# Gated cross-attention with two expert layers: the same calls on five engines in another written-out order

## The reference

```python
x = x + tanh(g_xattn[0]) * L0_xattn(layernorm(x), ctx)
x = x + tanh(g_ffn[0])   * L0_ffn(layernorm(x))
x = x + tanh(g_xattn[1]) * L1_xattn(layernorm(x), ctx, ctx)
x = x + tanh(g_ffn[1])   * L1_ffn(layernorm(x))

# L0_xattn: one head, both directions, and a gate
char2sub = softmax(Qc @ Ks.T / 16) @ Vs
sub2char = softmax(Qs @ Kc.T / 16) @ Vc
gate = sigmoid(concat(char2sub, sub2char) @ Wg.T + bg)
out  = gate * char2sub + (1 - gate) * sub2char
# L0_ffn: the best of 8 experts, each a 256x256 matrix
out  = (x @ expert_w[top1].T + expert_b[top1]) * max(softmax(x @ router_w.T + router_b))
# L1_xattn: 16 heads of 16 with rotary positions on q and k, then Wo
# L1_ffn: the best 2 of 8 experts, gelu(x @ w_fc.T) @ w_proj, weighted by a softmax over the two
```

## Time and profile before

| | before |
|---|---|
| median of three executions | 536.92 us |
| the three | 531.25, 536.92, 536.98 us |
| profiled execution | 531.52 us |
| its span | 530.2 us |
| mean granted clock of PE | 0.941 |
| PE busy | 469.8 us (89%) |
| VectorE, ScalarE busy | 346.1, 335.1 us |
| GpSimd busy | 280.8 us |
| DMA | 65.33 MB |

### The profile page before, as it was taken

One profiled execution on the slowest core, in us unless ns is written; L12 is line 12 of the kernel. 1 busy time (PEld: TensorE's weight loads), 2 busy tenths in 40 slices (PEclk: granted clock), 3 DMA queues, 4 the chain that ended last, 5 costly groups with the idle time before them and its releaser, 6 DMA issues.

```text
span 530.2 us, 11126 instructions
## 1 busy us (share of the span) xinstructions
PE 469.8 (89%) x3888; PEld 413.9 (78%) x3888; DVE 346.1 (65%) x865; ACT 335.1 (63%) x691; POOL 280.8 (53%) x362
## 2 busy tenths in 40 slices
PE   3999999999999674767886799999999999999996
PEld 3999999999888573636664558788788888878896
DVE  5576676787567557552645676868656695976475
ACT  3388788876758223322254578878867768687833
POOL 2236564575533876445366756837668184423154
PEclk9999999999999957777899579999999999999999
DMA  4679600015667415788768225051220602002001
GB/s 144 210 259 385 241 22 2 22 61 159 211 199 209 157 61 174 193 231 263 197 197 207 56 89 152 1 162 42 69 95 1 180 4 101 22 3 83 1 20 41
DMA packets 42635, 65.33 MB, mean 123 GB/s; under 512 B 6098, under 2 KB 23764, under 8 KB 42580
## 3 DMA queue, kind: packets, MB, share of 16 engines
q1 hardware_dynamic: 41044, 60.42, 37.4%
q0 software_dynamic: 1536, 4.20, 2.6%
HBM read 30.13 MB, written 17.43 MB: 90 GB/s over the span
## 4 chain that ended last, share of the span: by engine, by line
PE 61%; SPq 10%; DMA 8%; DVE 6%; issue 6%; POOL 5%; ACT 4%; POOLq 0%; DVEq 0%; ACTq 0%
PE psum L378 13%; PE psum L380 11%; PE psum L379 11%; SPq L2992 7%; PE psum L385 4%; PE psum L606 4%; PE psum L594 4%; DMA xs<-slots_d 3%; PE psum L577 3%; DMA st<-parts 3%; PE psum L543 2%; DMA y_d<-ys 2%; PE psum L510 1%; ACT PT L1346 1%; PE psum L419 1%
## 5 line engine op out<-in xcount | busy, mean ns | idle before, releaser
L2161 DVE TENSOR_REDUCE mpad<-psum 128x4 f32<-128x1024 f32 x64 | 76.4, 1220 | 23.9 <-PE psum L577 23.7
L1346 ACT ACTIVATE PT<-psum 128x1024 f32<-128x1024 f32 x64 | 63.7, 1026 | 17.6 <-PE psum L594 14.5
L2692 POOL TENSOR_TENSOR wA<-stage,wA 128x512 fp32r<-128x512 f32 x32 | 41.2, 1288 | 59.7 <-ACT wA L1393 57.1
L2230 DVE SCALAR_TENSOR_TENSOR xall<-psum,gat,xall 128x256 f32<-128x256 f32 x112 | 46.6, 474 | 9.7 <-PE psum L380 7.3
L577 PE MATMUL psum<-st 48*128 48x256 f32 x256 | 28.8, 331 | 12.3 <-DMA st<-parts 9.6
L378 PE MATMUL psum<-wB,wA 128*128 128x256 f32 x128 | 39.0, 304 | 0.1
L378 PE MATMUL psum<-x4h,wB 128*128 128x256 f32 x128 | 37.9, 296 | 0.1
L606 PE MATMUL psum<-PT,vv 128*32 128x256 f32 x512 | 36.0, 401 | 1.5 <-ACT PT L1346 1.5
L577 PEld LDWEIGHTS psum<-st 48*128 48x128 f32 x256 | 19.7, 202 | 21.9 <-DMA st<-parts 11.1
L2638 POOL TENSOR_SCALAR nm<-mv 128x2 f32<-128x2 f32 x32 | 7.7, 239 | 53.4 <-DVE mv L1926 41.8
L380 PE MATMUL psum<-x4h,wB 128*128 128x256 f32 x128 | 35.8, 280 | 0.0
(11 more groups left out here) (277 smaller groups left out, 1745.4 us busy)
## 6 DMA issues: line engine op xcount, KB each, us to landing
st<-parts SPq DMA_DIRECT2D x96, 128.0 KB, 3.1
wt<-exp_d SPq DMA_DIRECT2D x30, 384.0 KB, 3.9
slots_d<-ys SPq DMA_DIRECT2D x3, 2304.0 KB, 17.5
stage<-mats_d SPq DMA_DIRECT2D x21, 256.0 KB, 3.1
cx<-ctx_d SPq DMA_DIRECT2D x16, 256.0 KB, 4.5
qr<-qp SPq DMA_DIRECT2D x32, 128.0 KB, 2.6
xs<-slots_d SPq DMA_DIRECT2D x30, 128.0 KB, 4.0
y_d<-ys SPq DMA_DIRECT2D x30, 128.0 KB, 3.8
```

Source lines behind the costliest of these rows:

```text
L1346: e.activation(PT[:, i:i + 2, :, :].rearrange("p a k n -> p (a k n)"), ps2("ST", b, j).rearrange("p a n -> p (a n)"), ACT.Exp, scale=0.25) ...
L2161: e.tensor_reduce(mpad[:, :, 0:16].rearrange("p t (o a) -> p t o a", a=8)[:, :, :, j], ps2("max", b, j).rearrange("p o (t n) -> p t o n", ...
L2230: e.scalar_tensor_tensor(out=xall[:, b, t, :], in0=ps("dn", b, x)[:, t * 256:(t + 1) * 256], scalar=gat[:, b % 2, t, x:x + 1], in1=xall[:, ...
L2692: e.tensor_tensor(hlo[:, i, :], stage[:, n % 4, :], hh[:, i, :].bitcast(F32), ALU.subtract).then_inc(h_lo, 1)
```

## The change

The same calls stand in the lists in another order on all five engines, and PE's calls write other PSUM banks, as follows from it. No function changes, and no call is added or taken out. The diff has some 2,000 lines of this kind; a few of them:

```diff
 # PE: the numbers at the end are banks
-            proj("t1", 0, 5)
-            ln_T("A", 1, 1)
-            proj("vs", 0, 2)
-            scores(1, 0, 3)
+            proj("t1", 0, 2)
+            proj("vs", 0, 3)
+            ln_T("A", 1, 4)
+            scores(1, 0, 5)
...
 # SP, the start
+            load("wv")
             zero_slots(0)
             zero_slots(1)
             zero_slots(2)
             zero_slots(3)
-            load_x(6)
-            load_ctx("A", 4)
             load_ctx("A", 5)
-            load("wk")
-            load("wv")
-            load_x(5)
-            load_x(7)
             load_ctx("A", 6)
+            load_ctx("A", 7)
             load_ctx("C", 0)
+            load("wq")
+            load_tile(1)
+            load("r")
             load_tile(0)
...
 # SP, tiles 20 to 24
             load_tile(20)
+            load_tile(21)
             store_tile(17)
-            load_tile(21)
+            store_tile(18)
             load_tile(22)
-            store_tile(18)
+            load("f3")
+            store_tile(19)
             load_ctx("C", 3)
-            store_tile(19)
             load_tile(23)
+            load_tile(24)
             store_tile(20)
             store_tile(21)
-            load_tile(24)
             store_tile(22)
             load_tile(25)
             stack(1)
```

More of the change, by code:

```diff
@@ L690, in tensor_program @@
             proj("vs", 3, 0)
[L691 to L704, removed]
-            P_T(0, 3, 2)
-            P_T(1, 3, 3)
-            proj("vs", 4, 5)
-            ln_T("B", 0, 6)
+            scores(0, 3, 1)
@@ L709, in tensor_program @@
+            PV(0, 2, 3)
+            PV(1, 2, 2)
+            proj("vc", 3, 3)
+            mix(1, 2)
+            scores(1, 3, 4)
+            ln_T("A", 4, 0)
+            proj("t0", 4, 5)
+            gate(2, 1)
+            P_T(0, 3, 2)
+            P_T(1, 3, 4)
+            proj("t1", 4, 6)
+            proj("vs", 4, 0)
+            ln_T("B", 0, 7)
+            mix(2, 1)
             PV(0, 3, 2)
+            route_B(0, 4)
+            ln_T("A", 5, 7)
             PV(1, 3, 3)
-            mix(2, 0)
@@ L740, in tensor_program @@
[L740 to L745, removed]
-            proj("vc", 6, 6)
-            PV(0, 5, 0)
-            PV(1, 5, 1)
-            scores(0, 6, 2)
+            proj("vc", 5, 7)
+            PV(0, 4, 0)
+            ln_T("B", 2, 1)
+            PV(1, 4, 2)
+            route_B(2, 1)
+            rank(1, 3)
+            ln_T("B", 3, 4)
+            scores(0, 5, 5)
+            scores(1, 5, 0)
@@ L750, in tensor_program @@
+            rank(2, 1)
+            route_B(3, 2)
+            proj("t0", 6, 3)
+            ln_T("A", 6, 0)
+            rank(3, 2)
+            gate(4, 1)
+            P_T(0, 5, 4)
+            P_T(1, 5, 0)
+            proj("t1", 6, 5)
+            proj("vc", 6, 6)
+            proj("vs", 6, 2)
+            PV(0, 5, 7)
+            PV(1, 5, 0)
+            scores(0, 6, 1)
+            scores(1, 6, 3)
             moe_T(0, 0)
-            moe_T(1, 3)
-            scores(1, 6, 5)
-            mix(4, 1)
@@ L754, in tensor_program @@
-            moe_T(2, 7)
+            moe_T(1, 4)
+            moe_T(2, 5)
             moe_w(0)
             moe_w(1)
+            moe_w(2)
             gate(5, 0)
-            moe_w(2)
             P_T(0, 6, 1)
[L760 to L764, removed]
+            mix(4, 2)
+            P_T(1, 6, 3)
+            proj("t0", 7, 4)
+            proj("t1", 7, 2)
+            moe_T(3, 1)
+            moe_T(4, 5)
@@ L765, in tensor_program @@
+            proj("vs", 7, 7)
             moe_w(3)
[L766 to L768 removed]
+            ln_T("A", 7, 2)
+            moe_T(5, 3)
             moe_w(4)
             moe_w(5)
[L771 to L775, removed]
+            PV(0, 6, 1)
+            scores(0, 7, 2)
+            PV(1, 6, 0)
+            moe_T(6, 1)
+            scores(1, 7, 3)
             moe_w(6)
[L777 removed]
+            mix(5, 0)
@@ L948, in tensor_program @@
+            c_max(3, 3, 6)
+            c_max(4, 3, 4)
+            d_down(2, 0, 1)
+            d_down(3, 0, 3)
+            c_wo(1, 0)
+            c_exp(2, 2, 6)
+            c_exp(3, 2, 4)
+            c_PV(0, 2, 3)
+            c_max(5, 3, 6)
+            ln_T("C", 6, 1)
+            c_PV(1, 2)
+            c_exp(4, 2, 4)
+            d_down(4, 0, 0)
+            c_exp(5, 2, 6)
+            c_exp(6, 2, 4)
             d_down(5, 0, 2)
-            ln_T("D", 1, 1)
+            c_exp(7, 2, 6)
@@ L2379, in vector_program @@
             mixed(5)
+            b_top(4)
             y_out(9)
+            y_out(10)
             gated(6)
-            y_out(10)
             P_lo(0, 7)
@@ L2393, in vector_program @@
             y_out(14)
+            b_top(5)
+            gated(7)
+            vv_init()
+            mixed(7)
             slots(4)
-            gated(7)
-            mixed(7)
             add_moe(0)
             c_stats(0)
+            st1_init()
             b_top(6)
-            vv0_init()
             b_top(7)
```

986 lines of the change are left out of this document (480 added, 506 removed).

## The result

The median after is 539.42 us (20 executions, 534.82 to 543.28), that of the kernel before, run beside it, 534.53 us (20 executions, 529.37 to 542.55). The ratio of the runs compared with each other is 1.0157, with an interval of 1.0127 to 1.0186; the two medians taken over all executions differ by less, 0.9%. So the change costs 5 to 8 us: less than 2%, and on the other side of nothing than I forecast. The profiled execution took 539.4 us, its span is 538.1 us: 7.9 us more than before, at a mean clock of 0.933 for 0.941.

The account below looks back on a forecast made before the run. PE was taken as bound up to about 172 us and from 327 us, between them waiting on VectorE, SP and DMAs. Terms 0 - 0.2 - 1.4 + 0.3 + 0 = -1.3 us off 536.92 gave 535.6 us, range 526.5 to 541.

Parts of the forecast that it names:

- from 0 to 172 us: First layer's attention, PE full: late zeroing and load of r both have cover, 0 us, bounds -0.3 and +3.
- Rival 1: First stretch: lost cover holds ScalarE's calls and costs +3 us, giving 540 us; chance 0.15.
- Rivals 2 and 4: 2: late landings hold ScalarE some 12 us, 548 to 549 us, chance 0.05; 4: nothing moves, 537 or 531 us, 0.15.
- Rival 3: Shorter PE gaps from 227 to 310 us raise the clock: 529.5 us, or under 526; chance 0.15.
- From 172 to 227 us: gate(7) ahead of rank(4) gains 0.6 us, vv memsets stick out 0.4: net -0.2 us, bounds -1.0 and +1.0.
- From 227 to 272 us: Path through SP to stack(1), which comes 1.4 us earlier: net -1.4 us, bounds 0 and -2.1.
- (a): PE's moe_w(18) ahead of moe_T(19): load_tile(21)'s xs moves from 235.83 us to about 234.4.
- (b): store_tile(18) ahead of load_tile(22) frees the buffer y_out(21) waited 2.12 us for: gain 1.1 us.
- (c): load_tile(24) ahead of two stores: 0.3 us more, so stack(1) comes 1.4 us earlier in all.
- From 272 to 327 us: c_exp(3, 0) behind c_PV(0, 0) costs +0.3 us; the 3.64 us wait for st<-parts and half clock after it stay.

Follow-up runs that it names:

- experiment 6, x2_pool: Changed kernel with only gate_B(1) moved back ahead of sum_diff(4) on GpSimd: 536.99 us, ratio 1.0034 to the kernel before.
- y1_both: Changed kernel with, on GpSimd, gate_B(1) back ahead of sum_diff(4) and rex_in(2) ahead of out_lo(1, 4): 538.07 us, ratio 1.0082 to the kernel before.
- Experiment 12: h2_head188 with, on SP, store_tile(20) ahead of load_tile(24) and load_tile(25) ahead of store_tile(22): 532.48 us, ratio 0.9973 to the kernel before.
- h2_head188: Splice on all five engines: order of the kernel before up to about 188 us, changed order after: 532.31 us, ratio 0.9949 to the kernel before.

## Why the prediction was wrong

**The step that failed** is the first sum, *from 0 to 172 us*: "In sum 0 for this stretch". It named two moves as the ones that matter, and both went as the sum says. The zeroing began at 45.38 us (I had 47) and was issued by 61.6 (65):

```profile
45.38 16.18 SPq L2935 DMA_DIRECT2D slots_d<-ys  x4
```

`load("r")` was issued at 125.65 us, and ScalarE's `w_hi("r")` at 130.06 waited for nothing. The page of waits has no new wait of ScalarE's for a load. From 40 to 80 us PE is busy 39.77 us, as it was. What I put at nothing without looking was the third kind of neighbour. I had read who stands in front of whom on one engine, and who waits for whom by a semaphore, and never which operations of two engines fall on the same time. `gate_B(1)` in front of `sum_diff(4)`, 1.0 us of unimportant work, had kept `sum_diff(4)` from starting until `alloc(0)` was through. Moved back, it gives back about three quarters of the loss (experiment 6). Against this stands y1_both, which has it back too and still lost 0.8%, with two shorter holds in `alloc(0)`. The rest of the 1.6% isn't traced to a cause: up to 120 us, ahead of the collision, PE is busy 109.95 us for 111.25 before, and its first wait for a weight is 8.8 us for 8.0. The upper bound of that stretch, 3 us, was also too low: the shift was 3.5 us when `alloc(0)` ended, and 5.8 by 188 us. In between lie waits for `xs` (3.6 us for 0.9 up to 188 us) and a clock that fell twice (0.60 from 124 to 128 us, 0.65 from 180 to 184 us), where before it was full up to 184 us.

**Rival 1** gave 540 us and the median is 539.42, but its reason is refuted: it was VectorE and not ScalarE that was held, and beside GpSimd's work and not by a load. That its number fits is luck. **Rivals 2 and 4** didn't come. **Rival 3** went the other way. Taking the time at half clock as twice the span times what the mean clock lacks of 1, before has 62.6 us (530.2 us at 0.941) and after 72.1 (538.1 at 0.933).

**From 172 to 227 us** (forecast -0.2): the memsets of `vv` did stand out, by 0.5 us where I had 0.4. PE's `mix(7)` began at 188.50, and `mixed(7)` 1.15 us after it, against 0.67 us before:

```profile
188.50 1.03 DVE L2122 MEMSET vv<- 128x512 f32 x2
189.65 0.71 DVE L1983 SCALAR_TENSOR_TENSOR xall<-psum,htg,xall 128x512 f32<-128x512 f32 x1
```

`mix(7)` waited 1.11 us for 2.45, so `gate(7)`'s move helped. The wait for `xB` I had at 4.0 us and it was 4.65. From `mix(7)` to tile 18 the shift grew from +5.8 to +7.3 us: 1.5 us of loss for a forecast 0.2 of gain, outside my bound of +1.0.

**From 227 to 272 us** (forecast -1.4): steps (a) and (b) held, and of (c) the gain of tile 24 came but did not reach `stack(1)`. Measured from tile 18's shift of +7.3, tile 21 is at +5.4 (1.9 us nearer, I had 1.4) and tile 24 at +5.6. VectorE's wait for `y_d<-ys` before `y_out(21)` is gone, as the earlier trace rows had it with 2.12 us:

```profile
238.90 0.42 DVE L2097 TENSOR_TENSOR ys<-psum,wt 128x256 f32<-128x256 f32 x1 [4.56 <-DMA y_d<-ys]
...
248.74 0.42 DVE L2097 TENSOR_TENSOR ys<-psum,wt 128x256 f32<-128x256 f32 x1 [0.52 <-PE psum L543]
```

The wait moved to `y_out(18)`, which stands for `store_tile(15)`, and there it did less harm. But behind tile 24 there are now three stores, and tile 25 and `stack(1)` stand behind them:

```profile
250.49 0.33 SPq L2952 DMA_DIRECT2D xs<-slots_d  x1
250.87 1.45 SPq L2958 DMA_DIRECT2D y_d<-ys  x3
253.32 0.35 SPq L2948 DMA_DIRECT2D wt<-exp_d  x1
...
254.75 7.70 SPq L2992 DMA_DIRECT2D st<-parts  x12
```

Tile 25 is at +6.8, and so is `stack(1)`: it came 0.5 us nearer to tile 18 and not 1.4. I wrote that `store_tile(22)` and tile 25 "stand between" and put no price on them. Experiment 12 gives none either.

**From 272 to 327 us** (forecast +0.3): the 3.64 us wait for `st<-parts` did not stay. Smaller ones took its place (2.04 us for `PT` at 292.01, 2.31 for `mpad` at 307.74), and the clock was no better. From `stack(1)` to the end the shift grew by 1.1 us, of which my terms had 0.3; the difference is inside my bounds and isn't traced.

**The second half as a whole.** My terms from 188 us on sum to -1.1 us. h2_head188 measures between -2.7 us (ratio 0.9949 of 530.6) and +1.7 (by medians, 532.31 less 530.59). That is no refutation of the term and no proof of it. The profiled execution of h2_head188 has a span of 531.1 us, 0.9 more than the one before, and doesn't show where a gain would arise.

**The absolute numbers.** The forecast of 535.6 us lay 3.8 us below the median and the range, 526.5 to 541.0, holds it. That is luck in two ways. The range had been widened for the spread of executions and for ScalarE's waits, and the sum started from 536.92 us, where the kernel before measures 534.53 now.

## What to carry to other kernels

Before an order is changed, lay the timelines of VectorE and GpSimd over each other at every serial chain of small VectorE operations that read only SBUF, and see which large GpSimd operation will now fall beside it; here rows of 0.2 us became rows of 3. A harmless call that stands between the two can matter as much as a wait. Which row is caught, and what that costs at the end, these runs could not foretell: several of the expectations above were missed on it, so such a move has to be measured. And where PE is full, ask for each bank who empties it: a late engine surfaced there, under the name of whatever it did next.

## What the runs showed of the hardware

- A VectorE operation that GpSimd keeps out of SBUF can wait for more than one of GpSimd's instructions in a row. Holds of 3.14, 3.13, 3.28, 3.27 and 3.22 us, each beside `sum_diff(4)`, whose two instructions take 1.3 us each, and 3.75 us for a cast of 128x2, are all longer than the one instruction; the cast stood beside three in a row. It is not always so: L2079 and L2080 in y1_both (1.14 and 1.29 us) and L2088 in x2_pool (1.20 us) came out after one instruction. In the changed kernel the cast was held for 1.20 us in one profiled execution and 3.73 us in the other.
- Held rows of `alloc(0)` that lasted over 3 us begin 0.5 to 0.7 us before GpSimd's first large row (119.02 and 119.53, 118.31 and 118.90, 121.03 and 121.69), while the last instruction of the scatter was still running. That one alone held nobody: in the kernel before L2068 took 0.22 us beside such a row. Whether GpSimd takes the port before its row begins, or the rows are that rough, isn't settled.
- Operations with a single input in SBUF were held too (the cast, L2044; the product with a scalar, L2069, for 1.28 us). Those with an input in PSUM weren't: L1970 took 0.69 us at 123.07 in the kernel before, wholly beside L2664.
- Which operation is caught depends on a few tenths of a microsecond: L2068, L2073, L2082, L2079 with L2080, or L2088 in kernels that differ by one or two calls. Why y1_both (ratio 1.0082) is so much worse than x2_pool (1.0034), from which it differs by one exchange, stays open beyond that.
- The time of one execution goes with PE's clock. Over all kernels here, executions of the same kernel differ by 0.24 us for each microsecond more at half clock (fitted over 208 executions). At an equal 70 us of it, the kernel before takes 532.8 to 534.7 us in three comparisons, the changed one 537.3 and 538.1. So some 3 to 4 us of the loss are there at equal clock, and the rest goes with it. That division rests on the fit and on no experiment.
